# Delta stage: first chunk's transfers on two queues with a semaphore per kind of row, and a shared final normalisation

## What is computed

```python
def _step(S, inp):
    q_t, k_t, v_t, g_t, b_t = inp
    S = S * jnp.exp(g_t)[..., None, None]
    v_eff = (v_t - jnp.einsum('bhk,bhkv->bhv', k_t, S)) * b_t[..., None]
    S = S + k_t[..., None] * v_eff[..., None, :]
    o_t = jnp.einsum('bhk,bhkv->bhv', q_t, S)
    return (S, o_t)
...
x = _layernorm(x + _L0_attn_ref(x, ...), axis=-1)
x = _layernorm(x + _L0_xattn_ref(x, ctx_1024, _lenS2, ...), axis=-1)
x = _layernorm(x + _L0_ffn_ref(x, ...), axis=-1)
```

## Time and profile before

| | |
|---|---|
| median of 3 runs (lowest, highest) | 1695.08 us (1692.74, 1695.62) |
| the profiled execution: its time, its span | 1701.81 us, 1700.0 us |
| mean granted TensorE clock | 0.951 |
| busy: PE, DVE, ACT, POOL | 1518.7, 1086.1, 725.2, 673.1 us |
| DMA: bytes, mean rate over the span | 176.62 MB, 104 GB/s |

### The profile page before, as it was taken

How to read it: one execution, slowest core, us unless ns; L and a number is a source line. 1 busy time by engine, 2 the same in 40 slices (tenths; PEclk the granted TensorE clock), 3 DMA queues, 4 the chain that set the end, 5 groups by cost and what they waited for, 6 DMA issues and landing times. The chain is left out here.

```text
span 1700.0 us, 30447 instructions
## 1 busy us (share of the span) xinstructions
PE 1518.7 (89%) x10698; PEld 1077.3 (63%) x10698; DVE 1086.1 (64%) x2352; ACT 725.2 (43%) x1573; POOL 673.1 (40%) x526
## 2 busy tenths in 40 slices
PE   6999954799999999967999999997899999999990
PEld 3555523688888888543667777676655666666660
DVE  4899875568788875440558777788656445444443
ACT  4877751234444444453555454552242222222224
POOL 1354446212333311001343566545555544444440
PEclk9999985789999999997999999999899999999995
DMA  3233447645655535153133124110733332332236
GB/s 102 92 126 134 161 140 195 165 119 156 158 152 152 128 99 191 40 186 105 37 100 105 60 81 146 51 38 1 264 61 39 47 49 45 45 50 45 45 41 204
DMA packets 186794, 176.62 MB, mean 104 GB/s; under 512 B 79623, under 2 KB 147771, under 8 KB 186523
## 3 DMA queue, kind: packets, MB, share of 16 engines
q1 hardware_dynamic: 167659, 148.90, 29.1%
q0 software_dynamic: 17024, 22.43, 8.0%
q10 hardware_dynamic: 1968, 3.41, 0.7%
HBM read 110.67 MB, written 64.01 MB: 103 GB/s over the span
## 5 line engine op out<-in xcount | busy, mean ns | idle before, releaser
L2491 POOL DMA_INDIRECT y<-vw,idx x71 | 125.3, 1765 | 190.1 <-DVE vw L2638 179.2
L622 DVE SCALAR_TENSOR_TENSOR conv_y<-conv_in,taps,conv_y 128x512 f32<-128x512 f32 x192 | 161.5, 850 | 25.3 <-ACT conv_y L470 20.6
L1876 PE MATMUL xQ<-late,last 128*128 128x512 f32 x256 | 128.5, 626 | 10.6 <-ACT late L2039 4.8
L2553 PE MATMUL xO<-late,aT 128*128 x568 | 136.0, 383 | 0.8 <-DVE vw L2636 0.8
L2532 PE MATMUL xS<-w_gu,kT 128*128 x288 | 129.8, 593 | 0.4 <-issue 0.2
L375 PE MATMUL ps_j<-xnT,w_qkv 128*128 128x512 f32 x256 | 123.5, 607 | 0.0
L1820 POOL TENSOR_TENSOR sc<-sc,den 128x1232 f32<-128x1232 f32 x32 | 72.0, 2250 | 113.5 <-DVE den L2296 112.4
L2553 PEld LDWEIGHTS xO<-late,aT 128*128 128x128 f32 x568 | 103.5, 192 | 12.6 <-issue 1.2
L2623 DVE TENSOR_TENSOR sc<-xS,last 128x512 f32<-128x512 f32 x107 | 73.5, 691 | 55.7 <-PE xS L2532 51.1
L2636 DVE TENSOR_TENSOR vw<-xO,late 128x256 f32<-128x256 f32 x71 | 30.1, 424 | 120.7 <-PE xO L2553 115.5
L1814 POOL TENSOR_TENSOR sc<-sc,madd 128x1232 f32<-128x1232 f32 x32 | 82.8, 2587 | 36.3 <-DVE sc L2278 36.3
(11 more groups left out here) (359 smaller groups left out, 3669.6 us busy)
## 6 DMA issues: line engine op xcount, KB each, us to landing
carried<-qkvg SPq DMA_DIRECT2D x64, 256.0 KB, 3.9
qkvg<-tok SPq DMA_DIRECT2D x4, 2048.0 KB
qkvg<-gate SPq DMA_DIRECT2D x8, 1024.0 KB
qks<-qkvg SPq DMA_DIRECT2D x32, 256.0 KB, 4.7
steps<-step SPq DMA_DIRECT2D x30, 256.0 KB, 4.4
qkvg<-carried SPq DMA_DIRECT2D x3, 2048.0 KB
vw<-even SPq DMA_DIRECT2D x4, 1232.0 KB
xin<-in_x SPq DMA_DIRECT2D x9, 512.0 KB, 10.0
```

Source lines behind the costliest of these rows:

```text
L622: y = nc.vector.scalar_tensor_tensor(conv_y[m % 4][:], conv_in[b][:, m, k:k + BT], taps[:, m, k:k + 1], conv_y[m % 4][:], ALU.mult, ALU.add)
L1876: mm = pe.matmul(Q[:], w_q[:, c, j * P:(j + 1) * P], x1T[:, c, :], start=c == 0, stop=c == KD - 1)
L2491: nc.gpsimd.indirect_dma_start(out=s["y"].rearrange("t p d -> (t p) d"), out_offset=bass.IndirectOffsetOnAxis(ap=x.idx[j % 8][:, 0:1], axi ...
L2553: mm = pe.matmul(x.pD[:, 0:D], x.hT[q][:, k, :], w_d[:, bass.ds(e, 1), k, :], start=k == 0, stop=k == FK - 1)
```

## The change

It does five things:

1. `qk_in[b]` becomes three semaphores per batch, `step_in`, `grow_in` and `keys_in`. The diagonal waits for no load any more, the turns for keys, the scans for step rows, `decayed` for growth rows, `key_ends` for keys. Loads are issued as step, keys, growth, each behind the last reader of its own buffer; for chunk 0 all step rows of a queue go ahead of its growth rows.
2. In chunk 0 ScalarE's queue takes half of the work: the odd `lanes` blocks, the loads of chunk 1 for batches 2 and 3, and the eight stores of X.
3. The empty images are stored at the stage's start; VectorE sets U and T to zero instead of GpSimd. The output weights move from the start to behind `U<-image` of chunk 0.
4. In chunk 0 VectorE does PQ ahead of the block inverses instead of behind them; GpSimd does `key_ends` ahead of `decayed`.
5. Final stage: of blocks 0 to 6 GpSimd normalises the last row and ScalarE three; of block 7 ScalarE normalises rows 0 and 1, VectorE rows 2 and 3, and the block is stored in two halves.

```diff
-        load_gates(queue, s, b * CHUNKS, rows[:, b], steps[:, b * H:(b + 1) * H], landed[b])
+        load_step(queue, s, b * CHUNKS, f.step[:, b * H:(b + 1) * H], f.step_in[b])
+    for b in batches:
+        load_growth(queue, s, b * CHUNKS, f.grow[:, b], f.grow_in[b])
...
-    queue.dma_start(step[:], s["step"].rearrange("(n k) j -> n k j", k=H)[tile].unsqueeze(0).broadcast_to([P, H, P])
-                 ).then_inc(landed, 16)
+class First:
+    def __init__(self, grow, step, keys, sem):
+        self.grow, self.step, self.keys = grow, step, keys
+        self.grow_in, self.step_in, self.keys_in = [[sem(f"{n}_in{b}") for b in range(BATCH)]
+                                                    for n in ("grow", "step", "keys")]
...
+        def diagonals_out(queue, c, par, some):
+            queue.wait_ge(pk_done, at(c, BATCH - 1))
+            for n in some:
+                part = slice(n * B0, (n + 1) * B0)
+                queue.dma_start(lanes[part].rearrange("u (r c) -> r u c", r=B0), PK_all[par][part, :, part]
+                                ).then_inc(lane_out, 16)
+        def inverses_out(queue, c, k):
...
+        def next_scores(queue, b, c):
+            queue.wait_ge(E_done, at(c, b))
+            load_step(queue, s, c + 1 + b * CHUNKS, step[b], step_in[b])
+            queue.wait_ge(qkT_done, at(c, b))
+            queue.wait_ge(ke_done, at(c, b))
+            load_keys(queue, s, c + 1 + b * CHUNKS, qk[b], keys_in[b])
+            queue.wait_ge(qkg_done, at(c, b))
+            load_growth(queue, s, c + 1 + b * CHUNKS, grow[b], grow_in[b])
...
-            def next_scores(b, c):
-                sp.wait_ge(qkT_done, at(c, b))
-                sp.wait_ge(qkg_done, at(c, b))
-                sp.wait_ge(ke_done, at(c, b))
-                sp.wait_ge(E_done, at(c, b))
-                load_gates(sp, s, c + 1 + b * CHUNKS, grow[b], step[b], qk_in[b])
-                load_keys(sp, s, c + 1 + b * CHUNKS, qk[b], qk_in[b])
...
-                    diagonals_out(c, par)
+                    diagonals_out(sp, c, par, range(NB) if c else range(0, NB, 2))
...
-                    empty_image()
-                    for b in G:
-                        next_scores(b, c)
+                    for b in FIRST:
+                        next_scores(sp, b, c)
...
-                    inverses_out(c, 1)
+                    inverses_out(sp, c, 1)
...
-                    inverses_out(c, 0)
+                    if c:
+                        inverses_out(sp, c, 0)
...
+                        output_weights()
...
+            empty_image()
...
-                pool.wait_ge(qk_in[b], c * 64 + 64)
...
+                pool.wait_ge(grow_in[b], c * 32 + 32)
...
-                        decayed(0, b, 0)
-                    for b in G:
...
+                    for b in G:
+                        decayed(0, b, 0)
...
-            for t in (U_all, T_all):
-                nc.gpsimd.memset(t[:], 0.0).then_inc(zero_set, 1)
...
+                if c == 0 and f == 6:
+                    diagonals_out(act, c, par, range(1, NB, 2))
+                    for b in SECOND:
+                        next_scores(act, b, c)
+                if c == 0 and f == 13:
+                    inverses_out(act, c, 0)
...
-                dve.wait_ge(qk_in[b], c * 64 + 64)
+                dve.wait_ge(step_in[b], c * 16 + 16)
...
+            def query_products(c, par):
+                for b in G:
+                    dve.wait_ge(qq_done, c * 2 + b // 2 + 1)
+                    nc.vector.tensor_tensor(flat(PQ[par][b]), M[b][:], flat(E[b]), ALU.mult).then_inc(pq_done, 1)
+            for t in (U_all, T_all):
+                nc.vector.memset(t[:], 0.0).then_inc(zero_set, 1)
...
+                    if c == 0:
+                        query_products(c, 0)
...
-                if f == 0:
-                    for b in G:
-                        dve.wait_ge(qq_done, c * 2 + b // 2 + 1)
-                        nc.vector.tensor_tensor(flat(PQ[par][b]), M[b][:], flat(E[b]), ALU.mult).then_inc(pq_done, 1)
+                if f == 0 and c:
+                    query_products(c, par)
...
-            for n in N:
+            for n in N[:-1]:
...
+                sp.wait_ge(z_last, n + 1)
...
-            sp.wait_ge(z_out, 16 * BLOCKS)
+            for k, done in ((1, z_rest), (0, z_done)):
+                sp.wait_ge(done, 1 if k else BLOCKS)
+                sp.dma_start(out_v[BLOCKS - 1][:, 2 * k:2 * k + 2], y[BLOCKS - 1][:, 2 * k:2 * k + 2, :]).then_inc(z_out, 16)
+            sp.wait_ge(z_out, 16 * BLOCKS + 16)
...
+            for n in N[:-1]:
+                pool.wait_ge(sh_done, n + 1)
+                t = BLK - 1
+                nc.gpsimd.tensor_scalar(y[n][:, t, :], y[n][:, t, :], rstd[n][:, t:t + 1], shift[n][:, t:t + 1], ALU.mult,
+                                        ALU.add).then_inc(z_last, 1)
...
-                for t in T:
+                for t in T[:-1] if n < BLOCKS - 1 else T[:2]:
...
+            n = BLOCKS - 1
+            dve.wait_ge(sh_done, BLOCKS)
+            for t in T[2:]:
+                z = nc.vector.tensor_scalar(y[n][:, t, :], y[n][:, t, :], rstd[n][:, t:t + 1], shift[n][:, t:t + 1],
+                                            ALU.mult, ALU.add)
+            z.then_inc(z_rest, 1)
...
-            s["first"] = (one("grows", [P, BATCH, 2, P]),
-                          one("steps", [P, BATCH * H, P]), one("qks", [P, BATCH, 2 * DK]),
-                          [sem(f"qk_in{b}") for b in range(BATCH)])
+            s["first"] = First(one("grows", [P, BATCH, 2, P]), one("steps", [P, BATCH * H, P]),
+                               one("qks", [P, BATCH, 2 * DK]), sem)
```

More of the change, by code:

```diff
@@ L694, in delta_stage @@
         of_batch = lambda t: [t[:, b * H:(b + 1) * H, :] for b in G]
-        grow_all, step_all, qk_all, qk_in = s["first"]
+        first = s["first"]
+        grow_all, step_all, qk_all = first.grow, first.step, first.keys
+        grow_in, step_in, keys_in = first.grow_in, first.step_in, first.keys_in
         gates = lambda c, b: s["gates"][:, c + b * CHUNKS]
@@ L831, in run, with output_weights @@
                         rest(f, c + 2)
+        def diagonals_out(queue, c, par, some):
[5 more added lines that the diff above has]
+        def inverses_out(queue, c, k):
+            t, out, back = ((X16, u_out, u_in), (XT16, t_out, t_in))[k]
+            queue.wait_ge(base_done, c + 1)
+            if c:
+                queue.wait_ge(back, c * 16)
+            else:
+                queue.wait_ge(img_set, 32)
+            for n in range(NB):
+                part, lo = slice(n * B0, (n + 1) * B0), n % (NB // 2) * B0
+                queue.dma_start(image[k, part, :, lo:lo + B0].rearrange("r u c -> u r c"),
+                                t[part, 0:LANE].rearrange("u (r c) -> u r c", r=B0)).then_inc(out, 16)
+        def next_scores(queue, b, c):
[6 more added lines that the diff above has]
+            load_growth(queue, s, c + 1 + b * CHUNKS, grow[b], grow_in[b])
         @block.sync
         def _(sp):
-            sp.dma_start(w_o[:], a["L0_attn_Wo"].rearrange("(h p) n -> p h n", p=P)).then_inc(weights_in, 16)
-            sp.dma_start(norm_w[:], a["L0_attn_norm_w"].rearrange("(p a) -> p a", a=1)).then_inc(weights_in, 16)
+            def output_weights():
+                sp.dma_start(w_o[:], a["L0_attn_Wo"].rearrange("(h p) n -> p h n", p=P)).then_inc(weights_in, 16)
+                sp.dma_start(norm_w[:], a["L0_attn_norm_w"].rearrange("(p a) -> p a", a=1)).then_inc(weights_in, 16)
             def load_values(b, c):
@@ L848, in empty_image @@
                     sp.dma_start(image[k], t[:]).then_inc(img_set, 16)
[L850 to L856, removed]
             def diagonals_in(c):
@@ L860, in diagonals_in @@
                 sp.dma_start(N16[:, 0:LANE], lanes).then_inc(n_in, 16)
[L862 to L869, removed]
-                    part, lo = slice(n * B0, (n + 1) * B0), n % (NB // 2) * B0
-                    sp.dma_start(image[k, part, :, lo:lo + B0].rearrange("r u c -> u r c"),
-                                 t[part, 0:LANE].rearrange("u (r c) -> u r c", r=B0)).then_inc(out, 16)
             def inverses_in(c, k):
@@ L988, in key_ends @@
             def key_ends(c, b, par):
+                pool.wait_ge(keys_in[b], c * 16 + 16)
                 if c >= 2:
@@ L1072, in new @@
                     for b in (FIRST, SECOND)[f - 1]:
-                        pe.wait_ge(qk_in[b], c * 64 + 64)
+                        pe.wait_ge(keys_in[b], c * 16 + 16)
                         if c:
@@ L2672, in final_stage @@
         y_in = sems("y_in")
+        z_last, z_rest = sem("f_z_last"), sem("f_z_rest")
         set_up, st_done, mv_done, sd_done, r_done, sh_done, z_done, z_out = [
```

20 lines of the change are left out of this document (12 added, 8 removed).

## The result

| | before | after |
|---|---|---|
| median of 12 runs (lowest, highest) | 1695.93 us (1691.56, 1702.36) | 1690.68 us (1686.76, 1695.87) |
| ratio, 95% interval | | 0.9967 (0.9954, 0.9979) |
| the profiled execution: its time, its span | 1701.81, 1700.0 us | 1689.83, 1687.7 us |
| mean granted TensorE clock of it | 0.951 | 0.957 |

Ratios leave out the two executions at a far lower granted clock, one of e9's (0.642, 2310.25 us) and one of before beside it (0.552, 2660.72 us).

What follows compares the result with a forecast made beforehand. The delta stage's start-up chain, mostly through SyncE's queue, and ScalarE in the final stage were taken as the bounds. Terms -9.5 and -2.6 gave -12.1 us, from a median of 1695.1 to 1683.0, range 1677 to 1690.

Steps and rivals of the forecast that it cites:

- Semaphores, steps first: Delta stage's start: diagonals and turns start at 255.8, scans and PK end at 266.3 instead of 271.2, -4.9 us.
- Empty images and lanes: Chunk 0: lanes stand behind the 2 MB store, landing near 269.5; N lands at 273.3 instead of 278.35, -5.0 us.
- Loads on two queues: Chunk 0: SyncE issues two batches, not four, and starts XT at 281.2 instead of 288.38, -7.2 us.
- X on ScalarE's queue: Chunk 0: XT and X issued together in 4.5 us; U goes back at 288.3 instead of 299.97, -11.7 us.
- Weights: Behind U of chunk 0: 1.9 us of issue ahead of the values; lanes of chunk 1 -9.7, taken as -9.5 us.
- Steady chunks: Later chunks: keys issued 1.2 us earlier, ahead of growth rows; gain 0, at best 2 us over six chunks.
- Final stage: Kernel's end: ScalarE does three rows, VectorE's 1.99 us leads; last issue 1693.05 instead of 1695.53, -2.6 us.
- The queues take turns: Rival on XT and X in chunk 0: issue takes 7.6 us together; gain 9.0, 1686.1 us; chance 0.12.
- Image stores cost what the early start won: Rival in chunk 0: N lands at 278.3 as before, -4.5 and -2.6 remain, 1688.0 us; chance 0.10.
- Chunk 1 waits elsewhere: Rival: something taken as hidden holds chunk 1's date, only -2.6 and little else is left, 1692 us; chance 0.05.
- More than the sum: Rival: chunk 0 quicker without TensorE's stand, lanes past the store, weights hidden; -16.6, 1678.5 us; chance 0.12.
- slower: Rival on ScalarE's queue: odd lanes behind the 2 MB store, key copies delayed; 1699.5 us with N at 290; chance 0.03.

Runs made afterwards that it cites:

- e9: All of the change but the second queue (in chunk 0 SyncE alone sends lanes, loads four batches, stores XT and X): 1694.15 us, 0.9986 of the kernel before.
- e1: The kernel before with only the final stage of the kernel after: 1694.90 us, 0.9978 of the kernel before.
- e7: The kernel before, unchanged, run again for a second profile: one run, 1702.83 us.
- e5: The changed kernel with GpSimd's diagonals of chunk 1 moved ahead of its 13 memsets, timed: 1689.82 us, 0.9974 of the kernel before.

## Why the prediction was right or wrong

Marks from the stage's start, after against before.

1. *Semaphores, steps first*: right from the stage's start on. The lanes start at 11.0 instead of 15.4, -4.4 (forecast -4.9). That the stage would start at 255.8 as before was wrong: the loads' new order costs 0.9 to 1.9 us ahead of it, a term that the prediction did not have. Zeroing cost 0.91 for each tile, the scans 1.62 each.
2. *Empty images and lanes*: **here it failed**. I took the 2 MB store as what would hold the lanes and N. It landed at 268.8 (forecast 269.5) and did not hold N: N was issued 6.0 us earlier than before. But N landed only 1.1 earlier, not 5.0. I had moved half the loads of chunk 1 to a queue where they no longer stand behind N, and priced only their issue. The row that should have warned me is N's own landing of 2.1 us before: quick because everything else waited behind it on SyncE's queue.
3. *Query products in the wait*: right, nothing. *GpSimd's side* was wrong: chunk 1's diagonals, begun earlier and priced at nothing, ran beside the blocks and stretched them by 2.1 us. The same pair was in the earlier trace rows: scans beside diagonals took 1.67 each, and with GpSimd idle they take 1.14 (four in 4.56 at 288.55 in the kernel after).
4. *Loads on two queues*: SyncE was free when the blocks were done, as forecast (XT's store 0.4 us after the copy began, 2.7 before). But its start moved by -1.2 instead of -7.2, for N's and the blocks' reasons alone.
5. *X on ScalarE's queue*: right. Issue side by side took 4.1 (forecast 4.5), T and U 0.38 apart, the second 64 products no longer stand. ScalarE's stand showed as forecast: its copies began at 292.87, PK came at 297.12, and the products started at 298.09, released by T after 0.17 us of stand: ScalarE's stand stayed hidden, with little to spare. U goes back 6.65 us earlier, not 11.7: the missing 5.05 is 4 from part 2 and 2.1 from the blocks, less 1.0 of small things.
6. *Weights*: 0.9 us of issue, not 1.9; the second load took 1.49 before and 0.51 here. Lanes of chunk 1: -5.5 instead of -9.5. The eight themselves took 6.3 us, 4.4 before.
7. *Steady chunks*: from those lanes to the last T 324.9 us; 326.2, 327.2 (e1) and 332.9 (e7) in the kernels without the change's delta stage, 322.9 to 326.4 in those with it. One or two us against the first two, inside the forecast of 0 to 2, but e7 shows how far one profile strays.
8. *Final stage*: right, -2.2 for -2.6. GpSimd's row took 0.56 us, under a third of its room.

By the marks the sum is -5.5 - 2.2 = -7.7, and the step at fault is the landing of N with the blocks behind it (part 2, and 3 for GpSimd). The loss ahead of the stage (0.9 to 1.9 us) and the gain in the steady chunks (one or two) nearly cancel. The timed gain is 5.2, its interval 3.6 to 7.8: the marks lie at its edge, and some 2.5 us are not accounted for one by one.

The 12.3 us between the spans of the two profiles can be split: +0.25 until GpSimd's end, +1.25 until the stage's start, -5.5 until the lanes of chunk 1, -1.3 until the last T, -4.8 from there to the final stage's first load, and -2.2. The 4.8 lie in code that the change does not touch. Without them the two profiles would lie some 7.5 apart.

The time follows the granted clock. In the 23 runs of before timed beside e1, it was 0.956 in the quickest (1691.67) and 0.946 in the slowest (1707.86), and a straight line through them gives 1.6 us per thousandth; through the 17 beside e5, 1.0. By these rates 3 to 5 of the 12.0 us between the two profiles go with the clock: 0.951 in before's, where those 17 runs had 0.9544 on average and a median of 1694.83. Whether the clock sets the time or both follow something else was not tried. The prediction had allowed for before's profile sitting above its median; that a gain worked out on it would carry over whole was an assumption.

The rivals. *The queues take turns* is refuted for the stores of XT and X: 3.78 and 4.10 us side by side would have been 7.6 in turn. That speaks, for these transfers, against the Trainium skill, page "Perfetto Trace Analysis", section "DMA Instruction — HWDGE (DVE, Sync)". The growth loads at the stage's start went no faster on two queues than on one (0.61 us each against 0.62), though in the earlier trace rows four of them had taken 1.6; whether the queues took turns there, or waited for something else, no run shows. The other rule (the Trainium skill, "DMA: Bandwidth & Descriptors", "Issuing engines are not separate DMA queues") I had used for half: it also says that transfers from all queues interleave on the same 16 DMA engines. The trace agrees, with N's 7.05 us against 2.1. *Image stores cost what the early start won* came near in the numbers (N as late as before, 1688.0 us; N landed 1.1 earlier, 1690.68) and had the wrong cause: the stores were harmless to N. *Chunk 1 waits elsewhere* had the nearest time, 1692, but its mechanism did not come: the lanes of chunk 1 moved by 5.5 us. *More than the sum* and *slower* did not come.

## What to carry to other kernels

When loads move to a second queue, ask what small transfer of the first queue they used to stand behind. Bulk loads behind the small one on its own queue did not slow it here; with another queue's in flight, 128 KB that a chain waits for took up to 11 us instead of 2. Try holding the other queue's bulk loads, and only those, until the small one has landed: with that, and GpSimd's diagonals ahead of its memsets, the kernel took 0.9943 of the time before, the best ratio of all, against 0.9967. Ask too what stands behind loads that are put in a new order: here a store that the next stage's start waited for. And read an early start on GpSimd as a change of neighbours for VectorE, not as free time.

## What the runs showed of the hardware

- A 128 KB load took 2.0 to 2.1 us with loads of the same queue behind it, and 5.5, 7.0, 7.2, 9.2 and 11.1 us with a second queue's row and key loads in flight; one program gave both 5.5 and 11.1.
- Eight stores of 16 KB on each of two queues were issued in 3.8 and 4.1 us side by side (3.8 alone). Four growth loads (64 KB broadcasts) on each took 4.8 and 4.9 us side by side, where one queue alone issues two in 1.24.
- VectorE's 128x256 operation on two SBUF tiles took 0.42 us alone, and up to 1.15 beside GpSimd's 128x512 operations; beside GpSimd's memsets 0.42.
- GpSimd scales and shifts 128x256 in 0.56 us, where ScalarE takes 0.50 to 0.53.
- Runs of one kernel on one chip lay 16 us apart (1691.67 to 1707.86) with the granted clock (0.956 to 0.946). Of the 12.3 us between the profiles of the two kernels, 4.8 lay in code that both share, so one profile of each cannot tell a gain of 5 us.
